# A fused triangle/MLP kernel: the MLP output's row-scale product moved from VectorE to GpSimd, through a copy by ScalarE

## The chip, the cores and the metric

The kernel runs on one core of a Trainium2 chip. The metric is the device time of one launch in microseconds (us), the median of several runs. The engines are called by the profile's names: PE (TensorE matmul; PEld is its weight load), DVE (VectorE), ACT (ScalarE), POOL (GpSimd) and SP (SyncE, which here only issues DMAs).

## What is computed

An image x of 192 x 192 tokens with 64 channels goes through four residual layers. Layers 0, 1 and 3 are triangle updates. Layer 2, where the change is, is an MLP on group-normalised input whose two matrix products take operands that are quantised row by row to fp8 values:

```
def _quantize_rowwise(x):
    scale = jnp.clip(jnp.max(jnp.abs(x), axis=-1, keepdims=True), 1e-12, None) / 448.0
    return (x / scale).astype(float8_e4m3fn), scale
def _fp8_linear(x, w):
    xq, sx = _quantize_rowwise(x)
    wq, sw = _quantize_rowwise(w)
    return (xq @ wq.T) * sx * sw.T
...
h  = layer_norm(x, ln_w, ln_b)            # x: group norm of the layer's input
ab = _fp8_linear(h, w1)                   # 64 -> 512
a, b = jnp.split(ab, 2, axis=-1)
g  = relu(a) * b                          # 256 hidden values a token
out = _fp8_linear(g, w2)                  # 256 -> 64
x  = x + out
```

The scale of a token (a row) is multiplied onto the finished product of the second linear layer; that multiplication is what the change moves.

## The kernel before

A tile is 128 partitions with 8 tokens of 64 channels each: 128x512 values of f32. There are 36 tiles. Each engine runs its own instruction stream, written as one function for each engine and ordered by hand; semaphores tie them together. In each stage of the kernel an engine calls `pipeline(eng, [(lead, f), ...])`. It goes through turns i = 0, 1, 2, ...; in turn i it calls every f in the order of the list, for tile i + lead. Lead -6 so means "six turns after the tile entered". There is no loop on the chip: all turns are written out.

The second half of the MLP layer has in turn i, engine by engine and in this order:

- PE: the hidden layer of token pair 0 of tile i (`hidden_layer`, L1294), the sum of tile i-7 over its rows into the bank SUM (L1131), pair 1, the first half of the output product of tile i-5 (`mlp_out`, L1305, into the one bank O_BANK), pair 2, the sum of squares of tile i-7 (L1131), pair 3, and the second half of the output product.
- ACT: relu of pair 0 (`relu`, L1064), the division by the row scales for four tokens of tile i-2 (`hidden_scale`, L1072, four instructions), relu of pair 1, an absolute value for the rounding (`hidden_abs`, L1079), relu of pair 2, the other four tokens, relu of pair 3, the other absolute value, and the square of the new x of tile i-6 (`square`, L970).
- DVE: the product relu(a) * b of pair 0 (`hidden_product`, L869), the product of the output with the row scales of tile i-6 (`mlp_update`, L922), the first rounding step of half 0 of tile i-3 (`hidden_add`, L905), pair 1, the row maxima of tile i-1 (`hidden_amax`, L878), pair 2, the row scale (L893), the second rounding step of half 0 (`hidden_round`, L914), the inverse scale (L899), the first step of half 1 (L905), pair 3, and the second step of half 1 (L914).
- POOL: the full scale of tile i-2 (`hidden_full_scale`, L549, 128x8), for tile i-6 the addition of the residual (`update_mlp`, L520), and the subtraction of a common anchor that prepares the next group norm (`shift_new`, L474).
- SP: the load of the residual of tile i-5, the store of tile i-6, and the DMA transpose of the rounded hidden values of tile i-3 (`transpose_hidden`, L409).

Some waits matter below. `hidden_scale` of tile t overwrites the buffer that `hidden_round` of tile t-2 reads (two buffers), so ACT's first call in turn i waits for DVE's last instruction in turn i-1. `hidden_product` of a pair waits for that pair's relu. `mlp_out` of tile t waits until O_BANK has been read for tile t-1.

Of the kernel before, what the change touches and what calls it, by code (L numbers as in the profile page):

```python
# [23 lines left out]
ALU = mybir.AluOpType  # L24
# [6 lines left out]
U = 8  # L31
# [75 lines left out]
def build(nc, x_in, weights, biases, norms, mask, mlp_norm, w1, w2, out, layers=4):  # L107
    with ExitStack() as ctx:
# [3 lines left out]
        def sem(name):  # L112
            return ctx.enter_context(nc.semaphore(name))
# [10 lines left out]
        def part(buf, lo, n, bufs=2):  # L124
# [34 lines left out]
        w_bias = work[:, 3840:3840 + ROW]  # L159
        gn_pair = work[:, 4352:4352 + 4 * C].rearrange("p (k e c) -> p k e c", k=2, e=2)  # L160
        xres_m, prod_m = part(work, 8192, ROW), part(wide, 17408 + TILES * ROW, ROW)
        wq_raw, wq_y, wq_magic, wq_added, wq_q = (wide[:, TILES * ROW + 768 * k:TILES * ROW + 768 * (k + 1)] for k in range(5))
# [85 lines left out]
         mlp_out_ready, mres_loaded, least_ready, sg_ready,  # L248
         s_apart) = [sem(f"sem_{k}") for k in range(82)]

# [207 lines left out]
        def _(pool):  # L458
# [50 lines left out]
            def token_rstd(l, side, t, b):  # L509
# [5 lines left out]
                    .then_inc(rstd_ready, 1)  # L515

            def update_mlp(l, t, b):
                pool.wait_ge(prod_ready, x_base(l) + t + 1)
                wait_free(pool, xnew_stored[b], tile_landed(X_STORES, l, t - 2, b))
                pool.tensor_tensor(xnew[:, b, :], prod_m[:, b, :], xres_m[:, b, :], ALU.add).then_inc(xnew_ready, 1)  # L520
# [30 lines left out]
            for l in range(layers):  # L551
                if l not in TRIANGLES:
                    mlp_weights()
                group_rstd(l)
                if l in TRIANGLES:
                    pipeline(pool, [(4, lambda t, b, r: scale(l, t, b, r), RING),
                                    (5, lambda t, b, r: centre(l, t, b, r), RING),
                                    (3, lambda t, b: token_rstd(l, 0, t, b))])
                    tail = [] if l == LAST else [(0, lambda t, b: shift_new(l, t, b))]
                    pipeline(pool, [(4, lambda t, b: token_rstd(l, 1, t, b))] + tail)  # L560
                else:
                    pipeline(pool, [(2, h_sigma)])
                    pipeline(pool, [(-2, hidden_full_scale, RING),
                                    (-6, lambda t, b: update_mlp(l, t, b)),
                                    (-6, lambda t, b: shift_new(l, t, b))])
# [3 lines left out]
        def _(dve):  # L569
# [346 lines left out]

            def mlp_update(l, t, b):
                dve.wait_ge(mlp_out_ready, t + 1)
                dve.wait_ge(sg_ready, t + 1)
                wait_free(dve, xnew_ready, x_base(l) + t - 1)  # L920
                dve.wait_ge(mres_loaded[b], landed(16, t, b))
                dve.tensor_tensor(tokens(prod_m[:, b, :]), tokens(ps[:, O_BANK, :]),  # L922
                                  sg_all[:, bass.ds(t, 1), :].rearrange("p o u -> p (o u)").unsqueeze(2).to_broadcast([P, U, C]),
                                  ALU.mult).then_inc(prod_ready, 1)

            for l in range(layers):
# [20 lines left out]
                else:  # L947
# [4 lines left out]
                    for b in range(2):  # L952
# [4 lines left out]
                    least_scales()  # L957
                    pipeline(dve, [pair(0), (-6, lambda t, b: mlp_update(l, t, b)),
                                   add(0), pair(1), (-1, hidden_amax, RING),
# [6 lines left out]
        def _(act):  # L966
# [92 lines left out]
            def relu(pp, t, b):  # L1059
# [5 lines left out]
                               ps[:, bank:bank + 2, 0:HID], ACT.Relu).then_inc(relu_ready, 1)  # L1065

            def hidden_scale(half, t, b, r):
                if half == 0:
                    act.wait_ge(hid_step, 3 * (t + 1))
                    wait_free(act, hid_q, 2 * (t - 1))  # L1070
                for u in range(HALF * half, HALF * half + HALF):
                    last = act.activation(scaled[:, b, u * HID:(u + 1) * HID], hidden[:, r, u * HID:(u + 1) * HID],  # L1072
                                          ACT.Copy, scale=rescale[:, b, u:u + 1])
                last.then_inc(hid_scaled, 1)
# [6 lines left out]
            for l in range(layers):  # L1081
# [24 lines left out]
                else:  # L1106
# [5 lines left out]
                    absolute = lambda half: (-2, lambda t, b: hidden_abs(half, t, b))  # L1112
                    pipeline(act, [pair(0), scale(0),
                                   pair(1), absolute(0),
                                   pair(2), scale(1),
                                   pair(3), absolute(1), (-6, lambda t, b: square(sum_base(l) + t, b))])


        @block.tensor
        def _(pe):  # L1120
# [177 lines left out]
            def mlp_out(l, half, t, b):  # L1298
                if half == 0:
                    pe.wait_ge(hqT_ready[b], 16 * (t // 2 + 1))  # L1300
                    wait_free(pe, prod_ready, x_base(l) + t)
                for u in range(HALF * half, HALF * half + HALF):
# [8 lines left out]
            for l in range(layers):  # L1311
# [15 lines left out]
                else:  # L1327
# [8 lines left out]
                    out_half = lambda half: (-5, lambda t, b: mlp_out(l, half, t, b))  # L1336
                    sums = lambda bank: (-7, lambda t, b: add_to_sums(t, sum_base(l) + t, b, (bank,)))
                    pipeline(pe, [pair(0), sums(SUM), pair(1), out_half(0),
# [54 lines left out]
```

## Time and profile before

| | us |
|---|---|
| median of 3 runs | 1777.76 (1776.29 to 1778.16) |
| the profiled execution | 1780.16 |
| its span from first to last instruction | 1778.4 |
| granted clock of PE, mean | 0.907 of full speed |
| busy: PE / DVE / ACT / POOL | 1331.0 / 1383.3 / 1167.7 / 1001.5 |

The layer's second half starts at about 1008 us of the span and ends at about 1395 us. Times in the rows are us from the start of the span. A busy share is an average over stages that have different limits, so it doesn't say by itself which engine sets the time of a stage.

### The profile page before, as it was taken

What the parts mean: (1) busy time and instruction counts of PE and PEld (TensorE: products, weight loads), DVE (VectorE), ACT (ScalarE), POOL (GpSimd) and SP (SyncE); (2) the same over time, 40 slices, a digit from 0 to 9 for tenths busy, and PEclk for the clock granted to TensorE, in tenths of its full rate; (3) what the DMA queues carried; (4) which work ended last, traced back from release to release, by engine and by line L of the source; (5) the groups of instructions that cost most, each with busy time, mean ns of one, the idle gap of its engine ahead of it and who ended that gap; (6) DMA issues with size and microseconds to landing.
All of it is one profiled execution on the core that took longest, in us unless ns stands there. A gap on an engine that the chain in (4) does not pass through costs nothing.

```text
span 1778.4 us, 30667 instructions
## 1 busy us (share of the span) xinstructions
PE 1331.0 (75%) x9712; PEld 797.9 (45%) x9712; DVE 1383.3 (78%) x3708; ACT 1167.7 (66%) x2680; POOL 1001.5 (56%) x701
## 2 busy tenths in 40 slices
PE   5558888798688879798899657666675577778765
PEld 1123337665433349565677323333333233337654
DVE  6978871598688851898599899999999577761598
ACT  2358881598588851898343377777776288871598
POOL 7379960387699920687455214444445687740354
PEclk8879999899899999899899858989999799998789
DMA  7025436377545553677244124444445334435477
GB/s 263 0 78 119 120 88 155 99 222 208 142 107 119 120 120 77 182 227 208 89 110 113 33 54 110 105 108 107 106 109 119 96 100 107 100 78 133 135 256 249
DMA packets 408833, 225.53 MB, mean 127 GB/s; under 512 B 343456, under 2 KB 343776, under 8 KB 408672
## 3 DMA queue, kind: packets, MB, share of 16 engines
q1 hardware_dynamic: 270240, 185.81, 38.7%
q10 hardware_dynamic: 138432, 37.76, 9.1%
q8 instruction: 78, 1.28, 0.3%
q14 instruction: 83, 0.68, 0.1%
HBM read 114.97 MB, written 66.06 MB: 102 GB/s over the span
## 4 chain that ended last, share of the span: by engine, by line
issue 28%; DVE 21%; POOL 21%; ACT 16%; PE 12%; DMA 1%; SPq 0%; POOLq 0%; ACTq 0%; DVEq 0%
ACT work L1012 12%; POOL ln_s L514 6%; DVE stats L725 5%; PE ps L1131 5%; POOL work L506 4%; POOL work L520 4%; PE ps L1248 4%; POOL work L474 3%; POOL sg_all L549 2%; PE ps L1160 2%; DVE pairs L783 2%; ACT work L1025 2%; DVE stats L809 1%; DVE work L641 1%; ACT work L994 1%
## 5 line engine op out<-in xcount | busy, mean ns | idle before, releaser
L514 POOL TENSOR_TENSOR ln_s<-ln_s,half_power 128x8 f32<-128x8 f32 x216 | 356.4, 1650 | 355.7 <-DVE ln_s L734 305.2
L1173 PE MATMUL ps<-wfold,work 64*128 64x320 f32 x1728 | 342.6, 488 | 98.8 <-DVE pairs L783 52.8
L1131 PE MATMUL ps<-work,ones 128*128 128x512 f32 x504 | 280.6, 673 | 59.8 <-ACT work L970 49.5
L1012 ACT ACTIVATE work<-pairs,ln_s 128x64 f32<-128x64 f32 x648 | 263.4, 497 | 19.1 <-DVE ln_s L741 19.1
L1012 ACT ACTIVATE work<-work,ln_s 128x64 f32<-128x64 f32 x576 | 212.4, 430 | 95.4 <-DVE ln_s L741 95.2
L1173 PEld LDWEIGHTS ps<-wfold,work 64*128 64x128 f32 x1728 | 139.0, 190 | 270.6 <-DVE pairs L783 133.1
L783 DVE TENSOR_TENSOR pairs<-ps,work 128x256 f32<-128x256 f32 x288 | 169.0, 597 | 63.3 <-ACT work L1025 58.3
L1025 ACT ACTIVATE work<-ps 128x384 f32<-128x384 f32 x432 | 194.4, 476 | 4.9 <-PE ps L1173 3.8
L1160 PE MATMUL ps<-ident,work 128*128 128x128 f32 x864 | 147.7, 298 | 47.2 <-DVE work L752 28.8
L994 ACT ACTIVATE work<-ps 128x512 f32<-128x512 f32 x216 | 129.2, 598 | 72.1 <-PE ps L1160 70.5
L1072 ACT ACTIVATE pairs<-pairs,rescale 128x256 f32<-128x256 f32 x288 | 122.5, 498 | 71.3 <-DVE work L914 71.3
L474 POOL TENSOR_TENSOR work<-work,anchor 128x512 f32<-128x512 f32 x108 | 139.4, 1291 | 52.0 <-PE ps L1131 40.0
L1248 PE MATMUL ps<-work 128*128 128x128 f32 x864 | 132.2, 302 | 45.3 <-ACT work L994 45.0
L1248 PEld LDWEIGHTS ps<-work 128*128 128x128 f32 x864 | 122.5, 211 | 90.6 <-ACT work L994 57.6
L1131 PEld LDWEIGHTS ps<-work,ones 128*128 128x128 f32 x504 | 88.0, 202 | 159.2 <-ACT work L970 76.8
L520 POOL TENSOR_TENSOR work<-pairs,work 128x512 f32<-128x512 f32 x36 | 75.9, 2109 | 142.6 <-DVE pairs L922 142.6
L790 DVE COPY pairs<-ps 128x576 f32<-128x576 f32 x48 | 35.5, 756 | 152.7 <-PE ps L1201 77.7
L1160 PEld LDWEIGHTS ps<-ident,work 128*128 128x128 f32 x864 | 105.2, 151 | 96.5 <-issue 73.3
L1294 PE MATMUL ps<-w1s,pairs 64*128 64x256 bf16 (+1 forms) x864 | 104.2, 358 | 49.2 <-DVE pairs L869 40.9
L506 POOL TENSOR_TENSOR work<-work,gn_rstd 128x512 f32<-128x512 f32 x108 | 137.2, 1272 | 5.5 <-DVE gn_rstd L678 5.5
L1037 ACT ACTIVATE pairs<-ps 128x576 f32<-128x576 f32 x48 | 30.9, 650 | 157.6 <-PE ps L1201 65.3
L778 DVE SCALAR_TENSOR_TENSOR pairs<-ps,mask_t,work 128x128 f32<-128x128 f32 x288 | 99.3, 428 | 44.5 <-ACT work L1025 43.3
(148 smaller groups left out, 2636.0 us busy)
## 6 DMA issues: line engine op xcount, KB each, us to landing
work<-x_mid SPq DMA_DIRECT2D x144, 256.0 KB, 2.9
gate_dram<-work ACTq DMA_DIRECT2D x108, 256.0 KB, 2.8
work<-gate_dram SPq DMA_DIRECT2D x108, 256.0 KB, 3.2
work<-in_x_in SPq DMA_DIRECT2D x72, 256.0 KB, 2.9
work<-x_nat SPq DMA_DIRECT2D x144, 128.0 KB, 3.0
x_mid<-work SPq DMA_DIRECT2D x72, 256.0 KB, 2.6
work<-pairs SPq DMA_DIRECT2D x96, 96.0 KB, 3.0
work<-pairs ACTq DMA_DIRECT2D x96, 96.0 KB, 3.2
```

The lines of the kernel that those rows point to most:

```text
L474: pool.tensor_tensor(tokens(shifted[:, b, :]), tokens(src), over_tokens(anchor[:]), ALU.subtract)\
L506: pool.tensor_tensor(tokens(normed[:, r, :]), tokens(normed[:, r, :]), over_tokens(gn_rstd[:]), ALU.mult)\
L514: pool.tensor_tensor(ln_s[:, b, RSTD, :], ln_s[:, b, VAR, :], half_power[:, 0:U], ALU.pow)\
L520: pool.tensor_tensor(xnew[:, b, :], prod_m[:, b, :], xres_m[:, b, :], ALU.add).then_inc(xnew_ready, 1)
L783: last = dve.tensor_tensor(dst[:, :, bass.ds(t * U + u0, 2)].rearrange("p k u -> p u k"), ps[:, bank:bank + 2, 0:VALUES], gates[:, u0:u0 + ...
L994: act.activation(xnT[:, b, :], ps[:, T_BANK + b, :], ACT.Copy, bias=1.0 / ROOT_C).then_inc(xnT_ready, 1)
L1012: last = act.activation(dst[:, r % dst.shape[1], u * C:(u + 1) * C], src, ACT.Identity, scale=ln_s[:, b, RSTD, u:u + 1], bias=ln_s[:, b, S ...
L1025: act.activation(sig[:, b, 2 * GATES * pair:2 * GATES * (pair + 1)].rearrange("p (e g) -> p e g", e=2), ps[:, bank:bank + 2, VALUES:PROJ], ...
L1131: last = pe.matmul(ps[:, bank, :], ones[:], src[:, b, :], start=first, stop=end, skip_group_check=True)
L1160: last = pe.transpose(ps[:, T_BANK + b, k * P:(k + 1) * P], src[:, k * P:(k + 1) * P], ident[:])
L1173: last = pe.matmul(ps[:, PAIR_BANKS[n % 3] + odd, 0:PROJ], xnT[rows, b, pair * P:(pair + 1) * P], wfold[rows, q, 0:PROJ], start=True, stop ...
L1248: last = pe.matmul(ps[:, b, k * P:(k + 1) * P], xnT[:, b, k * P:(k + 1) * P], w_out, start=True, stop=True)
```

## The change

DVE's `mlp_update` is deleted. In its place ACT copies the output's bank to a new pair of SBUF buffers, `mlp_sum` (`move_mlp_out`), right after the relu of pair 0; POOL multiplies the copy with the row scales (`mlp_product`) ahead of `update_mlp`. PE's `mlp_out` now waits for ACT's copy of the tile before. The wait for the residual's load goes from the product to the addition. ACT's square and PE's two sums are called one turn later for each tile (lead -7 and -8).

```
+        mlp_sum = part(wide, 14336, ROW)
...
+            def mlp_product(l, t, b):
+                pool.wait_ge(mlp_moved, t + 1)
+                pool.wait_ge(sg_ready, t + 1)
+                wait_free(pool, xnew_ready, x_base(l) + t - 1 if t > 1 else 0)
+                pool.tensor_tensor(tokens(prod_m[:, b, :]), tokens(mlp_sum[:, b, :]), over_channels(sg_all[:, t, :]), ALU.mult)\
+                    .then_inc(prod_ready, 1)
...
             def update_mlp(l, t, b):
                 pool.wait_ge(prod_ready, x_base(l) + t + 1)
+                pool.wait_ge(mres_loaded[b], landed(16, t, b))
...
                     pipeline(pool, [(-2, hidden_full_scale, RING),
+                                    (-6, lambda t, b: mlp_product(l, t, b)),
                                     (-6, lambda t, b: update_mlp(l, t, b)),
                                     (-6, lambda t, b: shift_new(l, t, b))])
...
-                    pipeline(dve, [pair(0), (-6, lambda t, b: mlp_update(l, t, b)),
+                    pipeline(dve, [pair(0),
                                    add(0), pair(1), (-1, hidden_amax, RING),
...
+            def move_mlp_out(l, t, b):
+                act.wait_ge(mlp_out_ready, t + 1)
+                wait_free(act, prod_ready, x_base(l) + t - 1 if t > 1 else 0)
+                act.activation(mlp_sum[:, b, :], ps[:, O_BANK, :], ACT.Copy).then_inc(mlp_moved, 1)
...
-                    pipeline(act, [pair(0), scale(0),
+                    pipeline(act, [pair(0), (-6, lambda t, b: move_mlp_out(l, t, b)), scale(0),
                                    pair(1), absolute(0),
                                    pair(2), scale(1),
-                                   pair(3), absolute(1), (-6, lambda t, b: square(sum_base(l) + t, b))])
+                                   pair(3), absolute(1), (-7, lambda t, b: square(sum_base(l) + t, b))])
...
                 if half == 0:
                     pe.wait_ge(hqT_ready[b], 16 * (t // 2 + 1))
-                    wait_free(pe, prod_ready, x_base(l) + t)
+                    wait_free(pe, mlp_moved, t)
...
-                    sums = lambda bank: (-7, lambda t, b: add_to_sums(t, sum_base(l) + t, b, (bank,)))
+                    sums = lambda bank: (-8, lambda t, b: add_to_sums(t, sum_base(l) + t, b, (bank,)))
```

## Rows read from the trace of the kernel before

**Rows 1.** The page: busy time of each engine over the whole span.
```profile
PE 1331.0 (75%) x9712; PEld 797.9 (45%) x9712; DVE 1383.3 (78%) x3708; ACT 1167.7 (66%) x2680; POOL 1001.5 (56%) x701
```

**Rows 2.** Stretches of the stage: us, busy (x instructions) by engine, PEclk, DMA.
```profile
1058.00:1347.00 289.00, 197.59 (x2205) 93.04 (x2206) 289.00 (x350) 224.02 (x438) 132.89 (x88) 0.91 0.46 107
1347.00:1395.00 48.00, 30.19 (x330) 16.73 (x329) 33.22 (x32) 20.22 (x37) 25.22 (x16) 0.89 0.56 133
```

**Rows 3.** Waits from 1070 to 1330 us: total us, times, longest.
```profile
ACT pairs L1072 <- DVE work L914: 53.4, 26, 2.3
...
POOL work L520 <- DVE pairs L922: 112.2, 27, 4.2
...
PE ps L1305 <- DVE pairs L922: 44.1, 26, 1.8
```

**Rows 4.** Timeline of DVE, turn 19: start, duration, what.
```profile
1186.45 0.68 DVE L869 TENSOR_TENSOR pairs<-ps,pairs 128x512 f32<-128x512 f32 x1
1187.06 0.68 DVE L922 TENSOR_TENSOR pairs<-ps,sg_all 128x512 f32<-128x512 f32 x1
1187.65 1.21 DVE L905 SCALAR_TENSOR_TENSOR pairs<-pairs 128x1024 f32<-128x1024 bf16 x1
1188.85 0.69 DVE L869 TENSOR_TENSOR pairs<-ps,pairs 128x512 f32<-128x512 f32 x1
...
1194.66 0.69 DVE L869 TENSOR_TENSOR pairs<-ps,pairs 128x512 f32<-128x512 f32 x1
1195.26 1.22 DVE L914 SCALAR_TENSOR_TENSOR work<-pairs 128x1024 bf16<-128x1024 bf16 x1
```

**Rows 5.** Timeline of ACT in the same turn.
```profile
1186.63 1.71 ACT L1072 ACTIVATE pairs<-pairs,rescale 128x256 f32<-128x256 f32 x4 [1.54 <-DVE work L914]
1188.25 0.57 ACT L1064 ACTIVATE pairs<-ps 128x512 f32<-128x512 f32 x1
...
1193.69 0.58 ACT L1064 ACTIVATE pairs<-ps 128x512 f32<-128x512 f32 x1
1196.57 1.71 ACT L1072 ACTIVATE pairs<-pairs,rescale 128x256 f32<-128x256 f32 x4 [2.31 <-DVE work L914]
```

**Rows 6.** Timeline of DVE, pair 1 in turns 4 and 5, before the first `mlp_update`.
```profile
1039.75 0.69 DVE L869 TENSOR_TENSOR pairs<-ps,pairs 128x512 f32<-128x512 f32 x1 [0.58 <-ACT pairs L1064]
...
1049.69 0.69 DVE L869 TENSOR_TENSOR pairs<-ps,pairs 128x512 f32<-128x512 f32 x1 [0.58 <-ACT pairs L1064]
```

**Rows 7.** Timeline of ACT and POOL in layer 0: a POOL instruction that ACT releases.
```profile
340.44 2.40 ACT L1012 ACTIVATE work<-pairs,ln_s 128x64 f32<-128x64 f32 x6
...
343.01 1.64 POOL L514 TENSOR_TENSOR ln_s<-ln_s,half_power 128x8 f32<-128x8 f32 x1 [1.14 <-ACT work L1012]
```

**Rows 8.** One line each: POOL instructions of 128x512; ns min/median/max.
```profile
L506 POOL TENSOR_TENSOR work<-work,gn_rstd x108: 1258/1272/1281, 98.7 to 1573.6; 128x512 f32<-128x512 f32 x108
...
L530 POOL TENSOR_TENSOR work<-mlp_wb,ident x1: 1042/1042/1042, 854.5 to 854.5; 128x512 f32<-128x512 f32 x1
```

**Rows 9.** Timeline, two places where POOL is at work when DVE starts.
```profile
344.61 1.28 POOL L474 TENSOR_TENSOR work<-work,anchor 128x512 f32<-128x512 f32 x1
...
345.18 0.73 DVE L741 SCALAR_TENSOR_TENSOR ln_s<-stats,ln_s 128x8 f32<-128x8 f32 x1
...
1364.03 2.18 POOL L520 TENSOR_TENSOR work<-pairs,work 128x512 f32<-128x512 f32 x1 [3.08 <-DVE pairs L922]
...
1365.12 2.18 DVE L914 SCALAR_TENSOR_TENSOR work<-pairs 128x1024 bf16<-128x1024 bf16 x1
```

**Rows 10.** Timeline of PE and ACT in turn 20, which starts at 1196.39.
```profile
1199.46 2.07 PE L1131 MATMUL ps<-work,ones 128*128 128x512 f32 x2
...
1204.42 0.59 ACT L1064 ACTIVATE pairs<-ps 128x512 f32<-128x512 f32 x1
```

**Rows 11.** Timeline of DVE at the stage's end.
```profile
1388.62 0.69 DVE L922 TENSOR_TENSOR pairs<-ps,sg_all 128x512 f32<-128x512 f32 x1 [3.59 <-PE ps L1305]
...
1394.73 0.69 DVE L656 TENSOR_REDUCE gn_s<-ps 128x32 f32<-128x512 f32 x1 [5.42 <-PE ps L1131]
```

More of the change, by code:

```diff
@@ L248, in build @@
          mlp_out_ready, mres_loaded, least_ready, sg_ready,
-         s_apart) = [sem(f"sem_{k}") for k in range(82)]
+         mlp_moved,
+         s_apart) = [sem(f"sem_{k}") for k in range(83)]
         x_loaded, gate_stored, xnew_stored, mres_loaded, qT_ready, hqT_ready = [
@@ L915, in hidden_round @@
                                          op0=ALU.max, op1=ALU.subtract).then_inc(hid_q, 1)
[L917 to L924, printed above, removed]
             for l in range(layers):
```

## The prediction, made before the changed kernel was run

> **What bounds the kernel now.** I read the page first, then the stage by stretches, then the waits in it, then one turn of each engine, and last the turns in which the moved instruction isn't there yet. Over the whole span DVE is busiest, with 78% [rows 1], which settles nothing for one stage. In the stretch of steady turns DVE is busy 289.00 of 289.00 us, ACT 224.02, PE 197.59 and POOL 132.89 [rows 2]. So DVE looks like the bound, and an instruction taken from it looks like pure gain. The waits already say otherwise: ACT waits 53.4 us in 26 turns, each time for `hidden_round` (L914), DVE's last instruction of a turn [rows 3]. Something goes round between the two.
>
> One turn shows it. DVE's L914 ends, and ACT starts its four scalings (1186.63), which last 1.71 us; then comes the relu of pair 1, 1188.25 to 1188.82 [rows 5]. DVE's product of pair 1 starts at 1188.85 [rows 4], 0.03 us after it. Ahead of it `hidden_add` runs from 1187.65 for 1.21 us, to 1188.86, so that no gap shows in DVE's records. Two paths end at the same moment: DVE's own (pair 0, update, add) and the one through ACT (L914, scalings, relu of pair 1). The turns before the first update tell which one sets the period. There DVE has no L922; it waits 0.58 us for the relu, and the product of pair 1 still comes every 9.94 us (1039.75, 1049.69) [rows 6]. In the steady turns the period is the same, by ACT's first scaling: 1186.63 to 1196.57 [rows 5]. So the loop is: pair 1 to L914 on DVE, four scalings and a relu on ACT, and back. It takes 9.94 us with and without the update, and nothing on it is removed.
>
> **The change, part by part.** All times here are in the turn that starts at 1186.45.
>
> *DVE loses L922.* One step is 1187.06 to 1187.65, about 0.60 us [rows 4]. It lies in front of the product of pair 1, which waits for the relu anyway. Gain in a steady turn: 0. It would be 0.60 if the path through ACT were gone [rows 4, 6].
>
> *ACT gains a copy of 128x512 out of PSUM.* The nearest row is its relu of the same form and source, 0.58 us [rows 5]. It stands between the relu of pair 0 (1193.69 to 1194.27) and the scalings, before which ACT is idle 2.31 us, 1.54 us in the turn before [rows 5]. PE's half of the output that it waits for comes earlier in the turn than it did, since PE no longer waits 1.7 us a turn (44.1 / 26) for L922 [rows 3]. The copy costs nothing while that idle time covers it; without the cover, 0.49 us of a turn. ACT's instructions overlap by 0.09 us in the records (1186.63 + 1.71 against 1188.25), so the copy runs from about 1194.18 to 1194.76.
>
> *POOL gains a product of 128x512.* POOL is busy less than half of the stretch [rows 2], so its throughput isn't the question. The question is when it runs. It starts once the copy is done. From an ACT instruction to the POOL instruction that it releases it took 0.17 us (340.44 + 2.40 to 343.01) [rows 7], so the product starts at about 1194.93. For its duration there are two rows: 1.27 us for a full stream with a scale repeated over the tokens, and 1.04 us for the single instruction whose second operand is repeated over the channels, as here, but whose first is repeated too [rows 8]. I take 1.27, because `mlp_sum` is a full stream as in the first; 1.04 stays as the lower bound. So it runs until about 1196.20.
>
> *What that collides with.* DVE's L914 is due at 1195.26 [rows 4], in the middle of it. Two places of the trace show what happens then [rows 9]. In layer 0 a DVE instruction of 128x8 with two operands from SBUF starts at 345.18, while L474 has been running since 344.61; it takes 0.73 us and ends at 345.91, 0.02 after POOL. At the end of our stage L914 itself starts at 1365.12 under an L520 that ends at 1366.21; it takes 2.18 us and not 1.22, and ends 1.09 us after POOL. DVE waits for all of POOL's instruction [rows 9]. So here L914 would end at 1196.20 + 1.09 = 1197.29 and not at 1196.48: 0.80 us later. It is the one instruction that ACT's scalings wait for, so the delay goes into the loop whole: scalings, relu of pair 1 and the rest of the turn shift by 0.80 us. Today no POOL instruction is in this place: L520 waits for L922, up to 4.2 us [rows 3], and comes when the last L914 is over.
>
> The price by its bounds: 0.57 us a turn with a product of 1.04 us. Upwards, the later POOL starts the dearer it is, until L914 is there first: a product that starts just before 1195.26 costs 1195.26 + 1.27 + 1.09 - 1196.48 = 1.14 us. From 1195.26 on it is free, since POOL waits and not DVE.
>
> The Trainium skill states this as a rule (SBUF — State Buffer, "Who interferes with whom"): VectorE with two SBUF inputs and GpSimd with reads share one port pair, and whoever starts first keeps it for the whole instruction. By that rule this change is a bad one if POOL is first; the trace agrees, with the 0.73 us above. For the product's length the skill (GPSIMD Engine Reference, "Instruction dispatch") gives a floor of about 2.5 cycles an element with two inputs, an estimate of 1.07 us at its 1.2 GHz; with that the sum below would come to about 1795 us.
>
> *How many turns.* The delay needs the relu of pair 0 to be over early. In 17 of the 29 steady turns from 1057.23 on it starts 7.23 us after the turn's start, as at 1193.69 [rows 5]; in 12 it starts up to 0.8 us later, as at 1204.42 in a turn that began at 1196.39. In that turn PE's sum of squares took 2.07 us and held up pair 3 and all of ACT behind it [rows 10]. A copy behind so late a relu would end at about 9.1 us in the turn, after L914 has started (8.81), and cost nothing. But in the changed kernel the first half of the output needn't wait 1.7 us for L922 [rows 3], and all that PE does behind it in the turn can move forward by about as much. So I expect the late turns to be rare and take 27 of 30 (the ends of turns 5 to 34).
>
> *The rest of POOL.* After the delayed L914 comes `update_mlp`, for 1.27 us, while `hidden_add` is due 0.60 us into the turn; it gets the port at about 1.2 and ends at about 2.3. The relu lets pair 1 start at 2.40 (1188.85 - 1186.45), so that is covered, by 0.1 us only. L474 follows under pair 1 and the maxima, which have at most one SBUF operand. No cost.
>
> *Squares and sums one turn later, waits, SP.* Same instructions, same number. POOL's L474 now waits for the sum of squares of this same turn, some 3 us in; it has until the scale product at 6.0. PE's bank is freed by the copy, earlier than by L922. The residual's load was issued a turn ahead and isn't late; SP's order is as before. No cost.
>
> *The end of the stage* (48.00 us [rows 2]). When no relu is left, ACT copies earlier and the port is contended all the time [rows 9]. Three turns have one POOL instruction more (1.27) and one DVE step less (0.60): +2.0. The last tile's chain to L656, 1388.62 to 1394.73 [rows 11], gets a copy, its signal and a product (0.58 + 0.17 + 1.27 + 0.08) for an L922 and its signal (0.76): +1.3. PE's last output doesn't wait for the tile before: -1.7. An earlier copy in turn 35: -0.3. Together +1.3, anywhere from -2 to +4.
>
> **The sum.** 27 x 0.80 = 21.6, and 1.3: 22.9 us more. The profiled execution took 1780.16 (span 1778.4), so it would be 1803.1. The median before is 2.4 lower than that execution, so I forecast 1801 us. Own range of this case: from 27 x 0.57 - 0 = 15 (1793) to 30 x 1.14 + 3 = 37 (1815).
>
> **Rivals.**
> 1. *POOL comes second (no change).* If copy, signal and waits take 0.33 us longer than I put them, L914 has the port already, the product waits behind it and nothing on the loop moves: 1775 to 1781 us, 1778 likeliest. For it: the margin is small, POOL now goes through three waits, and 12 late turns exist. Against it: every one of the row times puts POOL first. It decides at a start of 8.81 us in the turn; I expect 8.48. Chance 0.12.
> 2. *Only the early turns collide:* PE's late turns stay as many as they are. 17.6 of 30 x 0.80 + 1.3 = 15.4: 1793, or about 1789 with the shorter product. Chance 0.10; still slower.
> 3. *DVE really is the bound (faster).* If the two paths weren't tied and the port weren't contended, 30 x 0.60 = 18 us would go: 1760 us. For it: DVE without a gap [rows 2]. Against it: the 9.94 us without L922 [rows 6]. It would need the relu of pair 1 to start 0.6 us earlier, and nothing in the change does that. Chance 0.07.
> 4. The forecast: 0.71.
>
> A difference under about 0.2% can't be told from none here. Slower 0.81, same 0.12, faster 0.07. The range must reach to the case of no change: 1776 to 1815.
>
> **What would show it.** In steady turns: a period of about 10.7 us; L914's second call at about 2.0 us and not 1.22, ending 1.09 us after POOL's product; that product right after ACT's copy and about 1.27 us long; a wait of some 0.1 us or more of DVE for L1064 ahead of pair 1; PE's wait for the bank gone; relus of pair 0 at 7.23 us in nearly all turns. What would make it wrong: a product that starts after L914 (period 9.94), a product as short as 1.04, or a `hidden_add` that ends later than 2.4 us and adds its own delay.

## The result and the profile after

The changed kernel takes 1794.57 us (median of 4 runs, 1793.9 to 1795.16) where the kernel before takes 1777.96 (4 runs): ratio 1.0099, 95% interval 1.0076 to 1.0122. It is slower by 16.6 us, about 0.9%. The forecast was slower, at 1801 us. The profiled execution took 1794.6 us with a span of 1792.8; before it was 1780.16 and 1778.4.

In the changed kernel's listing the lines have moved. L880 is the product relu(a) * b (L869 before), L925 `hidden_round` (L914), L916 `hidden_add` (L905), L1066 the relu (L1064), L1079 the scalings (L1072), L530 `update_mlp` (L520), L476 `shift_new` (L474), L559 the full scale (L549). New are L523, POOL's product, and L1072, ACT's copy.

The first view is the busy time of two stretches by engine, in the columns of [rows 2]: from turn 4 to turn 35 (31 turns), and from there to the first instruction of the next group norm. Before:

```profile
1037.36:1345.49 308.13, 208.56 (x2300) 97.80 (x2298) 306.98 (x372) 237.74 (x463) 134.97 (x89) 0.88 0.45 104
1345.49:1394.73 49.24, 30.27 (x330) 16.84 (x330) 34.46 (x34) 21.55 (x40) 25.37 (x16) 0.90 0.55 129
```

After:

```profile
1037.31:1359.35 322.04, 222.35 (x2298) 103.35 (x2297) 318.04 (x342) 250.09 (x492) 167.41 (x120) 0.83 0.45 100
1359.35:1408.50 49.15, 33.67 (x336) 18.82 (x334) 33.25 (x27) 25.31 (x47) 31.46 (x22) 0.83 0.56 128
```

All of it is in the 31 turns: 322.04 - 308.13 = 13.91 us of the span's 14.4. The end of the stage is as long as before. DVE has 30 instructions fewer in the 31 turns and is busy 11 us longer.

The timeline of one turn of the changed kernel, DVE first (it answers to [rows 4]), with the start of the next:

```profile
1182.27 0.68 DVE L880 TENSOR_TENSOR pairs<-ps,pairs 128x512 f32<-128x512 f32 x1
1182.87 1.68 DVE L916 SCALAR_TENSOR_TENSOR pairs<-pairs 128x1024 f32<-128x1024 bf16 x1
1184.65 0.69 DVE L880 TENSOR_TENSOR pairs<-ps,pairs 128x512 f32<-128x512 f32 x1
...
1190.46 0.68 DVE L880 TENSOR_TENSOR pairs<-ps,pairs 128x512 f32<-128x512 f32 x1
1191.06 1.70 DVE L925 SCALAR_TENSOR_TENSOR work<-pairs 128x1024 bf16<-128x1024 bf16 x1
1192.68 0.68 DVE L880 TENSOR_TENSOR pairs<-ps,pairs 128x512 f32<-128x512 f32 x1
```

ACT in the same turn, to be held against [rows 5]:

```profile
1182.43 1.70 ACT L1079 ACTIVATE pairs<-pairs,rescale 128x256 f32<-128x256 f32 x4 [2.29 <-DVE work L925]
1184.04 0.57 ACT L1066 ACTIVATE pairs<-ps 128x512 f32<-128x512 f32 x1
...
1189.48 0.59 ACT L1066 ACTIVATE pairs<-ps 128x512 f32<-128x512 f32 x1
1189.96 0.60 ACT L1072 ACTIVATE pairs<-ps 128x512 f32<-128x512 f32 x1
```

And POOL:

```profile
1188.29 1.11 POOL L559 TENSOR_TENSOR sg_all<-amax_scale,sx_all 128x8 f32<-128x8 f32 x1 [2.21 <-DVE amax_scale L904]
1190.64 1.04 POOL L523 TENSOR_TENSOR pairs<-pairs,sg_all 128x512 f32<-128x512 f32 x1 [1.24 <-ACT pairs L1072]
1191.76 2.13 POOL L530 TENSOR_TENSOR work<-pairs,work 128x512 f32<-128x512 f32 x1
```

Read them together. ACT's copy ends at 1190.56, POOL's product starts at 1190.64 and ends at 1191.68. L925 starts at 1191.06, in the middle, and takes 1.70 us instead of 1.22: it ends at 1192.76, 1.08 after POOL, close to the 1.09 of [rows 9]. The next turn starts 10.41 us after this one. No row says that DVE waits; its waiting for the port is inside the duration of L925, and counts as busy. (Alone L925 takes 1.22 us, so of the 0.62 us that POOL still had to run 0.48 is lost.) Behind it `update_mlp` (L530) has to wait until L925 is through, and `hidden_add` (L916, 1.68 instead of 1.21) for L530; that second wait is covered by the relu of pair 1, which ends at 1184.61, 0.04 us before the product of pair 1 starts.

### The profile page after: what moved, and what is told of

Its sections match the earlier page's. It is cut to its first block, busy times and chain, and to the rows that moved or that the text cites. A ratio compares the mean times of both kernels' runs of the same rounds, so it can differ in the third digit from the quotient of the medians.

```text
span 1792.8 us, 30700 instructions
## 1 busy us (share of the span) xinstructions
PE 1348.3 (75%) x9712; PEld 805.5 (45%) x9712; DVE 1393.2 (78%) x3672; ACT 1184.3 (66%) x2716; POOL 1040.2 (58%) x737
## 4 chain that ended last, share of the span: by engine, by line
DVE 29%; ACT 24%; issue 21%; PE 12%; POOL 12%; DMA 1%; SPq 0%; ACTq 0%; DVEq 0%; POOLq 0%
ACT work L1014 11%; POOL ln_s L516 6%; DVE work L925 5%; ACT pairs L1079 5%; PE ps L1138 5%; DVE stats L736 5%; POOL work L508 4%; PE ps L1255 4%; DVE pairs L916 3%; PE ps L1167 2%; DVE pairs L794 2%; ACT work L1027 2%; DVE stats L820 1%; ACT pairs L1086 1%; ACT work L996 1%
## 5 line engine op out<-in xcount | busy, mean ns | idle before, releaser
L1138 PE MATMUL ps<-work,ones 128*128 128x512 f32 x504 | 284.7, 682 | 59.9 <-ACT work L972 49.4
L476 POOL TENSOR_TENSOR work<-work,anchor 128x512 f32<-128x512 f32 x108 | 140.9, 1304 | 96.6 <-PE ps L1138 86.6
L1301 PE MATMUL ps<-w1s,pairs 64*128 64x256 bf16 (+1 forms) x864 | 110.6, 375 | 98.5 <-DVE pairs L880 90.1
L1079 ACT ACTIVATE pairs<-pairs,rescale 128x256 f32<-128x256 f32 x288 | 122.4, 498 | 78.9 <-DVE work L925 78.9
L501 POOL TENSOR_TENSOR work<-work,gn_mean 128x512 f32<-128x512 f32 x102 | 130.0, 1274 | 0.2 <-ACT work L1014 0.2
```

What stands on the lines that cost most here:

```text
L476: pool.tensor_tensor(tokens(shifted[:, b, :]), tokens(src), over_tokens(anchor[:]), ALU.subtract)\
L1138: last = pe.matmul(ps[:, bank, :], ones[:], src[:, b, :], start=first, stop=end, skip_group_check=True)
```

## The experiments

They ran on four chips, each time with the kernel before beside them. The kernel before had medians there of 1776.6 to 1780.5 us, and its runs scattered from about 1772 to 1785 with three at 1799 to 1802, more than in the first comparison (1776.3 to 1778.5). There is one profile of it, that of the first comparison, and the traces of the experiments are held against that one. The parts outside this stage, where the code is the same, differ from profile to profile by several us: turn 4 starts between 1033.4 and 1038.6 us, in e3_late1 at 1045.9. So the period of a turn and the length of the 31 turns (turn 4 to turn 35) in each trace are the finer measure, and the median with its ratio to the kernel before is the check. All results in one table; the expectations and readings follow.

| run | usual turn, us | 31 turns, us | median, us | ratio to before (95%) |
|---|---|---|---|---|
| before | 9.94 | 308.1 | 1777.96 | |
| changed | 10.42 | 322.0 | 1794.57 | 1.0099 (1.0076 to 1.0122) |
| e1_hold | 9.94, two of 10.1 | 308.4 | 1774.62 | 0.9981 (0.9964 to 0.9999) |
| e2_one_token | 9.94 | 308.1 | 1772.56 | 0.9962 (0.9943 to 0.9981) |
| e3_late1 | 10.51, two of 10.8 | 325.4 | 1799.46 | 1.0107 (1.0075 to 1.0139) |
| e4_late3 | 10.71 | 330.5 | 1802.98 | 1.0117 (1.009 to 1.0144) |
| e10_late6 | 9.94, two of 10.78 | 310.0 | 1782.43 | 1.0019 (0.9989 to 1.0049) |
| e5_no_product | 10.77, one of 9.93 | 331.6 | 1795.24 | 1.0101 (1.0064 to 1.0138) |
| e6_leads | 10.42 | 322.2 | 1791.16 | 1.0077 (1.0049 to 1.0105) |
| e7_relu_before | 9.87, some 10.4 | 308.6 | 1776.1 | 0.9987 (0.9971 to 1.0003) |
| e8_hold_relu | 9.79, four of 10.1 to 10.9 | 305.0 | 1774.03 | 0.9985 (0.9952 to 1.0018) |
| e12_before_relu_pe | 9.87 | 304.7 | 1777.11 | 1.0002 (0.9985 to 1.0019) |
| e9_window | 9.26 to 10.45 | 296.2 | 1778.14 | 0.9996 (0.9964 to 1.0027) |
| e11_window_pe | 9.27, some 9.73 | 290.8 | 1764.16 | 0.9909 (0.9877 to 0.994) |

**Is it the collision? The same work, started later.**

```
             def mlp_product(l, t, b):
                 pool.wait_ge(mlp_moved, t + 1)
+                pool.wait_ge(hid_q, 2 * min(t + 3, TILES))
```

> The changed kernel with one more wait: POOL's product of tile i-6 also waits until hidden_round's last half of the turn before is done. Same instructions, only a later start. Theory (port collision: the product starts 8.37 us into the turn, before hidden_round is due at 8.80, and delays it by 0.47 us): the product starts about 0.1 us into the next turn, hidden_round takes 1.22 us again, the period is 9.94 us instead of 10.42, and the time is about 1780 us. Rival (more work on POOL and ACT, or the longer chain copy, product, addition sets the time): 1794 us or more, since the chain becomes longer still.

Timeline of DVE and POOL in one turn; here L881 is the product relu(a) * b, L926 `hidden_round`, L917 `hidden_add`, L524 POOL's product.

```profile
1201.72 1.21 DVE L926 SCALAR_TENSOR_TENSOR work<-pairs 128x1024 bf16<-128x1024 bf16 x1
1202.86 0.68 DVE L881 TENSOR_TENSOR pairs<-ps,pairs 128x512 f32<-128x512 f32 x1
1203.46 1.74 DVE L917 SCALAR_TENSOR_TENSOR pairs<-pairs 128x1024 f32<-128x1024 bf16 x1
1205.26 0.69 DVE L881 TENSOR_TENSOR pairs<-ps,pairs 128x512 f32<-128x512 f32 x1
...
1203.07 1.04 POOL L524 TENSOR_TENSOR pairs<-pairs,sg_all 128x512 f32<-128x512 f32 x1 [3.01 <-DVE work L926]
```

L926 is back at 1.21 us and the turn at 9.94. The product now delays `hidden_add` instead (1.74 us), and this costs nothing, since pair 1 waits for the relu. Two turns are the exception: POOL's product starts 0.50 us into them and not 0.21, `hidden_add` ends behind the relu, and they take 10.08 and 10.10 us. Why POOL starts later there isn't known. One wait more makes the changed kernel about as fast as the one before (0.9981, upper end of the interval 0.9999). The slowdown is the product's place in time and not its work, nor the longer chain.

Nor is it PE's clock, which was lower in the changed kernel's 31 turns than before (0.83 against 0.88). With the held product it is as low, 0.82, in the columns of [rows 2]:

```profile
1033.78:1342.15 308.37, 221.68 (x2312) 103.45 (x2311) 305.69 (x343) 249.97 (x492) 163.77 (x118) 0.82 0.47 104
```


**Was DVE the bound before? Its product cut to one token of eight.**

```
-                dve.tensor_tensor(tokens(prod_m[:, b, :]), tokens(ps[:, O_BANK, :]),
-                                  sg_all[:, bass.ds(t, 1), :].rearrange("p o u -> p (o u)").unsqueeze(2).to_broadcast([P, U, C]),
+                dve.tensor_tensor(tokens(prod_m[:, b, :])[:, 0:1, :], tokens(ps[:, O_BANK, :])[:, 0:1, :],
+                                  sg_all[:, bass.ds(t, 1), 0:1].rearrange("p o u -> p (o u)").unsqueeze(2).to_broadcast([P, 1, C]),
                                   ALU.mult).then_inc(prod_ready, 1)
```

> The kernel before, with DVE's product of the output and the row scales cut from 8 tokens to 1 (128x64 instead of 128x512): seven of eight tokens get no product of their own, stale values are added. DVE gains about 0.45 us a turn. Theory (the loop hidden_round, scalings, relu of pair 1 sets 9.94 us): period 9.94 us, 1777 us, within 0.2% of before, and DVE waits about 0.4 us for the relu of pair 1. Rival (DVE, which shows no gap, is the bound): 30 x 0.45 = 13 us faster, 1764 us.

Timeline of DVE, with the kernel before's line numbers:

```profile
1202.55 0.68 DVE L869 TENSOR_TENSOR pairs<-ps,pairs 128x512 f32<-128x512 f32 x1
1203.15 0.21 DVE L922 TENSOR_TENSOR pairs<-ps,sg_all 128x64 f32<-128x64 f32 x1
1203.28 1.21 DVE L905 SCALAR_TENSOR_TENSOR pairs<-pairs 128x1024 f32<-128x1024 bf16 x1
1204.94 0.69 DVE L869 TENSOR_TENSOR pairs<-ps,pairs 128x512 f32<-128x512 f32 x1 [0.45 <-ACT pairs L1064]
```

What DVE saves comes back as a wait of 0.45 us for the relu, and 31 turns take 308.1 us, as before. The period is as the theory said, the total isn't: the median is 0.4% lower, where 0.2% at most was expected. The profiled execution is 4.4 us shorter than the one before. 2 us of this are at the stage's end (47.3 us against 49.2), where no relu is left to wait for. 3.7 us come ahead of turn 4, where the two programs are the same, so they aren't the product's. The rival's 13 us in the turns aren't there.

**The law of the price: the product later by one, three and six small ACT copies.** They stand in ACT's idle time ahead of the copy: one in the first run, and `range(3)` in the second.

```
             def move_mlp_out(l, t, b):
...
+                for k in range(1):
+                    act.activation(mlp_late[:, k, :], half_power[:], ACT.Copy)
                 act.activation(mlp_sum[:, b, :], ps[:, O_BANK, :], ACT.Copy).then_inc(mlp_moved, 1)
```

> The changed kernel with one ACT copy of 128x8 (some 0.2 to 0.3 us, in ACT's idle time) ahead of the copy of the output. Theory: the product starts later by that much but still ahead of hidden_round, and the delay of hidden_round grows by exactly as much: start in the turn + 1.04 + 1.09 - 10.03 us. With 0.2 us: period 10.62 us, 6 us above the changed kernel, about 1800.5. Rival (the work counts, not its place): 1794.6, no change, since ACT is idle there.

> The same with three ACT copies of 128x8, so that the product starts about 0.6 us later, at about 8.97 us of the turn, after hidden_round (8.80). Theory: POOL now waits for DVE and not DVE for POOL; the period falls back to 9.94 us and the time to about 1780, although ACT does more work than in the run with one extra copy. Rival: equal to or slower than the changed kernel, 1794.6 or more.

Such a copy costs ACT only 0.10 us, half of what I had put, so three of them didn't reach the point at which the sign turns. Both runs fell on the line that the theory draws. (10.03 is the time in the turn at which `hidden_round` ends when nothing holds it, 8.81 + 1.22.) One copy: the product starts 8.46 us into the turn, which makes 8.46 + 1.04 + 1.09 - 10.03 = 0.56 us more than 9.94; measured 10.51. In two of its turns the product starts at 8.75, and they take 10.79 and 10.80. Three: 8.66, 0.76, and 10.71. The second expectation (back to 9.94) failed because the copies were too short to pass `hidden_round`, so six followed, of 128x4 (`range(6)`, with `half_power[:, 0:4]` as the source):

> The changed kernel with six small ACT copies (128x4) ahead of the copy of the output. One such copy moved the product by 0.1 us, three by 0.3, and both made the turn longer by as much (10.51 and 10.71 us); neither passed hidden_round. Six should move the product's start from 8.37 to about 8.97 us, behind hidden_round's start at 8.80. Theory (who starts first keeps the port): the period falls from 10.71 with three copies to 9.94 us with six, and the 29 turns between tile 6 and tile 35 shrink by 22 us. Rival (each ACT copy simply lengthens the turn): 11.0 us, 10 us slower than with three.

Timeline of DVE, then POOL:

```profile
1204.85 1.22 DVE L926 SCALAR_TENSOR_TENSOR work<-pairs 128x1024 bf16<-128x1024 bf16 x1
1205.98 0.69 DVE L881 TENSOR_TENSOR pairs<-ps,pairs 128x512 f32<-128x512 f32 x1
1206.58 1.47 DVE L917 SCALAR_TENSOR_TENSOR pairs<-pairs 128x1024 f32<-128x1024 bf16 x1
1208.38 0.69 DVE L881 TENSOR_TENSOR pairs<-ps,pairs 128x512 f32<-128x512 f32 x1 [0.34 <-ACT pairs L1067]
...
1204.99 1.97 POOL L524 TENSOR_TENSOR pairs<-pairs,sg_all 128x512 f32<-128x512 f32 x1 [1.80 <-ACT pairs L1075]
```

The product starts at 1204.99, 0.14 us after L926. Now POOL waits (1.97 us for an instruction of 1.04), L926 takes 1.22, and the turn is 9.94 us. From three copies to six ACT's added work doubles and the 31 turns shrink from 330.5 to 310.0 us. Of the 1.9 us above 308.1, 1.7 are two early turns of 10.78, in which there is no square on ACT yet and the product starts 0.2 us earlier, at 8.74 us, 0.07 ahead of L926: the dearest place that was measured.

**Less work on POOL: the product left out.** The row scales are not applied; the addition reads ACT's copy.

```
             def update_mlp(l, t, b):
-                pool.wait_ge(prod_ready, x_base(l) + t + 1)
+                pool.wait_ge(mlp_moved, t + 1)
...
-                pool.tensor_tensor(xnew[:, b, :], prod_m[:, b, :], xres_m[:, b, :], ALU.add).then_inc(xnew_ready, 1)
+                pool.sem_inc(prod_ready, 1)
+                pool.tensor_tensor(xnew[:, b, :], mlp_sum[:, b, :], xres_m[:, b, :], ALU.add).then_inc(xnew_ready, 1)
...
-                                    (-6, lambda t, b: mlp_product(l, t, b)),
...
             def move_mlp_out(l, t, b):
                 act.wait_ge(mlp_out_ready, t + 1)
-                wait_free(act, prod_ready, x_base(l) + t - 1 if t > 1 else 0)
+                wait_free(act, xnew_ready, x_base(l) + t - 1 if t > 1 else 0)
```

> The changed kernel without POOL's product: the addition of the residual reads ACT's copy directly, so the row scales are left out. POOL has 1.04 us less to do in a turn. Theory: the addition of 1.27 us is now the instruction that starts before hidden_round, at about 8.37 us, and delays it by 8.37 + 1.27 + 1.09 - 10.03 = 0.70 us: period 10.65 us, 7 us SLOWER than the changed kernel (1801) although an instruction is gone. Rival (POOL's added work costs the time): faster than the changed kernel, toward 1778.

Timeline of POOL and DVE; L531 is the addition, L925 `hidden_round`:

```profile
1214.04 1.27 POOL L531 TENSOR_TENSOR work<-pairs,work 128x512 f32<-128x512 f32 x1 [1.36 <-ACT pairs L1072]
...
1214.34 2.04 DVE L925 SCALAR_TENSOR_TENSOR work<-pairs 128x1024 bf16<-128x1024 bf16 x1
```

In the turns the theory holds: with an instruction less the period rises from 10.42 to 10.77, because the longer addition has taken the product's place (8.50 + 1.27 + 1.09 - 10.03 = 0.83 above 9.94). One turn escaped: in it the addition started at 8.79 us, POOL was the one that waited (2.36 us), and the turn took 9.93. The total doesn't show it: 1795.24 us, where about 1801 was expected. Against the changed kernel's profile the 31 turns are 9.5 us longer and the stage's end is 3.2 shorter (45.9 us against 49.15), where one POOL instruction less a tile counts. Another 5.2 us are saved ahead of turn 4 and behind the stage, where the code is the same, so the total says nothing about the product; only the period is evidence here.

**The other edit: squares and sums at their old leads.**

```
-                                   pair(3), absolute(1), (-7, lambda t, b: square(sum_base(l) + t, b))])
+                                   pair(3), absolute(1), (-6, lambda t, b: square(sum_base(l) + t, b))])
...
-                    sums = lambda bank: (-8, lambda t, b: add_to_sums(t, sum_base(l) + t, b, (bank,)))
+                    sums = lambda bank: (-7, lambda t, b: add_to_sums(t, sum_base(l) + t, b, (bank,)))
```

> The changed kernel with squares and sums at their old leads (-6 and -7). Theory: they are off the loop; period 10.42 us, 1794.6 within 2 us (one turn less at the end may give 1 us). Rival: the wait of POOL's shift for the sums of the same turn (it shows 1.3 us a turn) costs time; then several us faster.

The period is the same 10.42 us, so the later squares and sums cost nothing in the turns. The median is 3.4 us below the 1794.57 of the first comparison, with overlapping intervals of the ratio; no clear effect. The profile has the stage's end 2.6 us longer (51.8 us against 49.15), where up to 1 us less had been expected, and 4 us less ahead of turn 4, where nothing was changed. With one profile of each the 2.6 us aren't shown to be the leads.

**Can the removed product be turned into time?** First the loop itself, without the change: ACT's relu of pair 1 ahead of the scalings.

```
-                    pipeline(act, [pair(0), scale(0),
-                                   pair(1), absolute(0),
+                    pipeline(act, [pair(0), pair(1), scale(0),
+                                   absolute(0),
```

> The kernel before with ACT's relu of pair 1 called before the first four scalings instead of behind them. Theory: this opens the loop; DVE's own path is then the bound, and it is only about 0.1 us a turn shorter than the loop (the product of pair 1 started 0.03 us after the relu and 0.09 us before the rounding step's recorded end): period 9.84 to 9.94 us, 0 to 3 us faster. Rival (the relu's place doesn't matter or its move delays the scalings): same or slower.

Then the same order of ACT on the changed kernel with the held product (the wait of e1_hold):

> The changed kernel with the held product (starts when hidden_round is done) and the relu of pair 1 ahead of the scalings. Theory: with the loop open DVE is the bound, but hidden_add now has to wait for POOL's product (about 0.15 to 1.2 us into the turn) and ends at about 2.3 us: period about 9.75 us, some 5 us faster than before (1772). Rival A (the full 0.6 us of the removed product is gained): 9.25 us, 1757. Rival B (a port wait elsewhere): 9.94 or more.

Both came out as forecast in most turns: 9.87 and 9.79 us. With the loop open DVE is the bound, and in e8 POOL's product makes `hidden_add` wait on what is now the path (1.73 us), so that most of the 0.6 is lost again. In seven turns of e7 (10.3 to 10.4 us) and two of e8 (10.6 and 10.9) the relu of pair 1 was late; on PE pair 1 stands behind the sum of the rows there, and e12 below, where it doesn't, has no such turn. Two more turns of e8 (10.1) have POOL's product 0.3 us later, as in e1. The totals moved by less than 0.2%, and the 5 us that were expected of e8 aren't in its median (1774.03, ratio 0.9985).

The last step removes the second collision. Two runs share these edits (the first line is in `mlp_product`), with squares and sums at -6 and -7:

```
+                pool.wait_ge(hid_added, min(2 * (t + 3) + 1, 2 * TILES))
...
-                    pipeline(dve, [pair(0),
-                                   add(0), pair(1), (-1, hidden_amax, RING),
+                    pipeline(dve, [add(0), pair(0), pair(1), (-1, hidden_amax, RING),
...
-                    pipeline(act, [pair(0), (-6, lambda t, b: move_mlp_out(l, t, b)), scale(0),
-                                   pair(1), absolute(0),
+                    pipeline(act, [pair(0), (-6, lambda t, b: move_mlp_out(l, t, b)), pair(1), scale(0),
+                                   absolute(0),
```

The second, e11_window_pe, changes PE's order as well:

```
-                    pipeline(pe, [pair(0), sums(SUM), pair(1), out_half(0),
+                    pipeline(pe, [pair(0), pair(1), sums(SUM), out_half(0),
```

> From the changed kernel: ACT's relu of pair 1 ahead of the scalings (opens the loop), DVE's order hidden_add, pair 0, pair 1, maxima, pair 2 (a stretch of about 4.0 us in which DVE has no instruction with two SBUF inputs), POOL's product held until that hidden_add is done, so that its three instructions (1.04 + 1.27 + 1.27 and gaps, 3.8 us) fit in the stretch; squares and sums at their old leads. Theory: DVE never waits for the port and is the bound without the removed product: period 9.25 us, 20 us less than the kernel before in 29 turns, about 1757 us where before has 1777. Rival A (another wait appears: PE's pair 1 late behind the sums, as in some turns of the run with the held product and the early relu): turns of 9.25 mixed with turns of 9.8 and more. Rival B (the last POOL instruction reaches into the row scale step): 9.3 to 9.5 us.

> As the run with the window, and PE computes pair 1 ahead of the sum of the rows. If late relus of pair 1 come from the sum standing in front of pair 1 on PE, all turns are 9.25 us and this one is the faster of the two by what the late turns cost; if not, the two are the same.

Timeline of e11_window_pe, DVE and then POOL:

```profile
1215.51 1.23 DVE L917 SCALAR_TENSOR_TENSOR pairs<-pairs 128x1024 f32<-128x1024 bf16 x1
1216.64 1.30 DVE L881 TENSOR_TENSOR pairs<-ps,pairs 128x512 f32<-128x512 f32 x2
1217.84 2.29 DVE L890 TENSOR_REDUCE tok<-pairs 128x8 f32<-128x2048 f32 x1
1220.03 0.70 DVE L881 TENSOR_TENSOR pairs<-ps,pairs 128x512 f32<-128x512 f32 x1
1220.63 0.17 DVE L905 SCALAR_TENSOR_TENSOR amax_scale<-tok,least_all 128x8 f32<-128x8 f32 x1
...
1216.87 1.05 POOL L524 TENSOR_TENSOR pairs<-pairs,sg_all 128x512 f32<-128x512 f32 x1 [4.14 <-DVE pairs L917]
1218.00 1.28 POOL L531 TENSOR_TENSOR work<-pairs,work 128x512 f32<-128x512 f32 x1
1219.36 1.28 POOL L476 TENSOR_TENSOR work<-work,anchor 128x512 f32<-128x512 f32 x1
```

POOL's three instructions run from 1216.87 to 1220.64, while DVE has only instructions with at most one SBUF operand, and end when L905, which has two, is recorded at 1220.63 with its usual 0.17 us. No duration in the turn is stretched on either side. The period is 9.27 us in 22 of the 31 turns; in seven it is 9.72 to 9.74, and in two 9.4, with POOL's product 0.28 us later. The run without PE's edit had the same 9.27 in its good turns but 18 longer ones (rival A of its expectation), and no gain in the median: 1778.14 us, where 1757 was expected. Its profile, the fastest of its ten executions, has the 31 turns 12 us shorter than before; where the slower executions lost this isn't recorded. With PE's edit: 1764.16 us, ratio 0.9909 (0.9877 to 0.994), faster than both kernels, but 7 us short of the 1757 that turns of 9.25 would have given. Its 31 turns are 17.4 us shorter than before, and the end of the stage is 1.9 us longer (51.15 us).

What of this comes from the product's move, and what from the reordering? The kernel before with the two reorderings of ACT and PE alone:

> The kernel before, with its product still on DVE, plus the two reorderings of the window run that have nothing to do with the product: ACT's relu of pair 1 ahead of the scalings and PE's pair 1 ahead of the sum of the rows. Theory: the loop is open and DVE is the bound with its product on it: every turn 9.87 us, 2 us less than before in 29 turns, about 1775 where before has 1777 to 1778; then 12 us or more of what the window run gains come from having the product off DVE. Rival (the reorderings alone make the gain): near the 9.27 us and 1764 of the window run.

Timeline of DVE: pair 0 of turns 5, 6 and 7, with the first `mlp_update` between the last two.

```profile
1043.32 0.68 DVE L869 TENSOR_TENSOR pairs<-ps,pairs 128x512 f32<-128x512 f32 x1
1052.59 0.68 DVE L869 TENSOR_TENSOR pairs<-ps,pairs 128x512 f32<-128x512 f32 x1
1053.19 0.68 DVE L922 TENSOR_TENSOR pairs<-ps,sg_all 128x512 f32<-128x512 f32 x1
1062.46 0.68 DVE L869 TENSOR_TENSOR pairs<-ps,pairs 128x512 f32<-128x512 f32 x1
```

The last turn before the first update takes 9.27 us, and each of the 29 with it 9.87. The median is unchanged (1777.11 us, 1.0002), though the 31 turns are 3.4 us shorter. So the reorderings of ACT and PE alone don't bring the window's gain: the window's 31 turns are 304.7 - 290.8 = 13.9 us shorter still. The two runs differ in DVE's order too, which wasn't tried alone. But with DVE's old order a turn without the product already takes 9.27 us, the window's period, so these 13.9 us come from having the product off DVE, once the loop is open and POOL out of the way. A step of 0.60 us less in 29 turns would be 17.4 us; the nine longer turns of e11 give back 3.5 of it.

## Why the prediction was right, point by point

- *The loop through L914, the scalings and the relu of pair 1 sets 9.94 us, and nothing on it is removed:* shown. With seven eighths of L922 gone (e2) and with all of it gone (e1) the turn stays 9.94. The late relu is what holds it: ahead of the scalings (e12) the turn falls to DVE's own 9.87.
- *POOL's product starts before L914 is due and delays it until 1.09 us after POOL's end:* shown by one and the same product started at six places. Starts at 8.37, 8.46, 8.66 and 8.74 us cost 0.48, 0.57, 0.77 and 0.84 us; at 8.96 and at 10.15 (0.21 into the next turn) they cost nothing.
- *The price of a turn, 0.80 us:* too high, by two terms. The product took 1.04 us (median of 36), the lower of the two rows in [rows 8] and not 1.27: the row whose second operand is repeated over the channels was the right one, whatever its first. And POOL started 0.08 us after ACT's copy, not 0.17 as in [rows 7]; with a copy that ended 0.02 us sooner than forecast this puts it at 8.37 and not 8.48. 0.80 - 0.23 - 0.11 = 0.46; measured 0.48, mostly.
- *How many turns, 27 of 30:* all 30. Not one relu of pair 0 was late in the changed kernel; all start at 7.22 or 7.23 us or, in the first turns, at 7.0. PE's wait for the bank (44.1 us in [rows 3]) is gone, as forecast; that this is what made the relus punctual was argued and not tried alone. In the two turns before the squares begin the product starts at 8.16 to 8.18 and costs 0.28. Sum: 2 x 0.28 + 28 x 0.475 = 13.9 us, the whole of 322.04 - 308.13.
- *The copy on ACT, the rest of POOL, leads and loads at no cost:* held in the turns. The copy lies in ACT's idle time (2.29 us before the scalings remain). `hidden_add` ends at 1184.55, 0.1 us ahead of the product of pair 1; this cover was thin, as said, and is the first to go once the loop is opened (e8).
- *The stage's end, +1.3 us:* measured -0.1 (49.15 against 49.24), inside the bounds given.
- *Total:* +22.9 forecast; +14.4 in the profiled executions and +16.6 in the medians. The mechanism and its place were right; the size of the product and of its release were not. The shorter product stood in the range as the lower bound (1793). Two smaller errors cancelled by luck: three turns too few (1.4 us) and an end of the stage put 1.4 us too long.
- *Of the rivals:* "POOL comes second" isn't this kernel, but it begins 0.44 us away (8.81 against 8.37): e10 is this case. "DVE is the bound" is false for both kernels and true for e12 and for the turns of 9.27 us in e11.

By the Trainium skill (SBUF — State Buffer, "Who interferes with whom") the engine that starts first keeps the shared port for its whole instruction; e4 and e10 agree with it: a product that starts 0.14 us ahead of L926 makes it wait, and one that starts 0.14 us behind it waits itself. The floor of about 2.5 cycles an element that the Trainium skill gives (GPSIMD Engine Reference, "Instruction dispatch"), an estimate of 1.07 us here at its 1.2 GHz, was nearer to the measured 1.04 than the row that I took. The measured time lies slightly below it, so as a floor it isn't exact here.

## What to carry to other kernels

An engine without a gap in the trace needn't be the bound: look for the turn in which the instruction in question is missing, and see whether the period changes (9.94 us with and without the update before; 9.87 against 9.27 in e12). Before work is moved to POOL, lay its start against the next DVE instruction that reads two operands from SBUF and feeds a loop; if POOL is just ahead, the move costs most of what POOL still has to run, every turn (0.48 of 0.62 us here), and one wait that holds it back, or a stretch of DVE instructions with at most one operand in SBUF, made it free here. Of the two rows for POOL's product the right one was the one whose second operand was repeated as in the new instruction.

## What the runs showed of the hardware that was not expected

- A blocked instruction is recorded as a longer one and counts as busy: `hidden_round` 1.70 us for 1.22, with no idle time before it. DVE's busy time rose by 11 us with 30 instructions fewer.
- An engine that waits for the port gets it ahead of the other's next instruction: L530 is recorded from 1191.76, 0.08 us after L523's end, but takes 2.13 us and ends at 1193.89, 1.13 us after L925, where an unhindered one takes 1.26. So it ran only after L925.
- The cost as a function of POOL's start is a saw tooth. Between starts at 8.74 and 8.96 us it falls from 0.84 us to nothing.
- POOL's product with a scale repeated over the channels takes 1.04 us for 128x512 values, its addition of two full tiles 1.26.
- An ACT copy of 128x8 or 128x4 is recorded with 0.20 us but pushes the next instruction back by 0.10 only.
- PE's clock reaches the turn once the rest is out of the way. In the seven turns of 9.73 us in e11 it is at its lower level from the start of the turn (`hidden_add`) on for 4.4 to 5.3 us. Turns that start at the lower level but have it for 3.5 us at most keep their 9.27, as do turns 4 and 6, lower throughout, in which PE has no sums yet. The columns are those of [rows 2]; the first stretch lies in a turn of 9.26 us, the second in one of 9.74:

```profile
1215.51:1220.50 4.99, 4.39 (x64) 2.31 (x62) 4.99 (x6) 4.96 (x12) 3.47 (x3) 1.00 0.77 161
1224.77:1229.76 4.99, 4.99 (x35) 2.75 (x34) 4.63 (x6) 3.88 (x8) 3.46 (x3) 0.50 0.72 156
```

The granted clock is 1.00 in the one (2.4 GHz) and 0.50 in the other (1.2 GHz). In the second PE is busy throughout, and the product of pair 2 starts 4.97 us into the turn, where it starts at 4.52 in the first: 0.45 of the 0.48 us by which the turn is longer. What PE did before the clock fell stands in its timeline:

```profile
1220.79 0.61 PE L1301 MATMUL ps<-w1s,pairs 64*128 64x512 bf16 x6 [0.38 <-DVE pairs L881]
1223.80 1.04 PE L1301 MATMUL ps<-w1s,pairs 64*128 64x512 bf16 x6 [2.40 <-DVE pairs L881]
```

It stood idle for 2.40 us, the clock fell at about 1223.2 in that gap, and the same matrix products took 1.04 us instead of 0.61. It came back at about 1230.1, when PE had been busy without a gap since 1223.80. In the changed kernel the mean granted clock of the 31 turns also fell, from 0.88 to 0.83, without any effect on the period: turn 18, with a mean of 1.00, and turns with 0.83 all take 10.41 or 10.42 us. What makes the clock fall wasn't tried.
